# Attention with a conditioned residual: in the last slots the products for the maxima come by pairs of heads

## What is computed

```python
h = _layernorm(x)
mod = jax.nn.silu(time) @ mod_w + mod_b
shift, scale, gate = jnp.split(mod, 3, axis=-1)
h = h * (scale + 1.0) + shift
qkv = (h @ w_qkv).reshape(B, T, 3, H, e).transpose(2, 0, 3, 1, 4)
q, k, v = (qkv[0], qkv[1], qkv[2])
q = _apply_rope(_layernorm(q, q_norm_w), position)
k = _apply_rope(_layernorm(k, k_norm_w), position)
scores = jnp.einsum('bhqe,bhke->bhqk', q, k) / jnp.sqrt(jnp.asarray(e, q.dtype))
attn = jax.nn.softmax(scores, axis=-1)
o = jnp.einsum('bhqk,bhke->bhqe', attn, v)
o = o.transpose(0, 2, 1, 3).reshape(B, T, D)
return x + o @ w_out * gate
```

## Time and profile before

| | |
|---|---|
| median of three runs | 1695.15 us (1694.68 to 1695.43) |
| profiled execution, its own time | 1697.0 us |
| its span, first to last instruction | 1694.8 us |
| TensorE busy (matmul) | 1633.6 us, 96% of the span |
| VectorE busy | 1238.2 us, 73% |
| ScalarE busy | 997.5 us, 59% |
| GpSimd busy | 977.5 us, 58% |
| mean granted TensorE clock | 0.986 of full speed |

### The profile page before, as it was taken

How to read it: one execution, slowest core, us unless ns; L and a number is a source line. 1 busy time by engine, 2 the same in 40 slices (tenths; PEclk the granted TensorE clock), 3 DMA queues, 4 the chain that set the end, 5 groups by cost and what they waited for, 6 DMA issues and landing times.

```text
span 1694.8 us, 31070 instructions
## 1 busy us (share of the span) xinstructions
PE 1633.6 (96%) x11846; PEld 960.7 (57%) x11846; DVE 1238.2 (73%) x1541; ACT 997.5 (59%) x1484; POOL 977.5 (58%) x769
## 2 busy tenths in 40 slices
PE   5979999999999999999999999999999999999887
PEld 3745565565555556566556555555656655655344
DVE  8767777777777777777777777777777777776453
ACT  3436665666666656566566666665656656666552
POOL 0525466566666665656656666666665665666452
PEclk9979999999999999999999999999999999999899
DMA  6024455546546455555555555654645555454563
GB/s 219 26 62 94 107 124 116 137 110 145 116 104 153 109 125 128 125 118 119 138 115 128 128 122 117 133 125 109 147 113 118 132 118 136 108 122 103 125 137 106
DMA packets 55417, 204.25 MB, mean 121 GB/s; under 512 B 6872, under 2 KB 6872, under 8 KB 39144
## 3 DMA queue, kind: packets, MB, share of 16 engines
q0 software_dynamic: 18144, 132.13, 38.6%
q1 hardware_dynamic: 37128, 70.14, 13.0%
HBM read 53.25 MB, written 16.88 MB: 41 GB/s over the span
## 4 chain that ended last, share of the span: by engine, by line
PE 91%; DVE 4%; issue 1%; ACT 1%; DMA 1%; SPq 0%; POOL 0%; DVEq 0%; ACTq 0%
PE Y L339 33%; PE O L447 13%; PE SA L428 13%; PE Y L357 10%; PE SM L396 6%; PE MB L379 3%; PE SA L432 3%; PE Y L462 3%; PE SA L331 2%; DVE cst L1053 1%; PE SA L406 1%; ACT probs L806 1%; DMA probs<-in_L_cond_w_qkv_dram 1%; DMA probs<-probs 1%; DVE wqkv_lo L1096 0%
## 5 line engine op out<-in xcount | busy, mean ns | idle before, releaser
L1288 POOL TENSOR_TENSOR probs<-probs 128x2048 f32<-128x2048 f32 x62 | 285.4, 4603 | 313.3 <-DMA probs<-probs 313.3
L1053 DVE TENSOR_REDUCE cst<-SM 128x2 fp32r<-128x1024 f32 x256 | 313.9, 1226 | 144.4 <-PE MB L396 142.6
L806 ACT ACTIVATE probs<-SM 128x1024 f32<-128x1024 f32 x256 | 263.0, 1027 | 137.9 <-PE SM L432 123.2
L1053 DVE TENSOR_REDUCE cst<-MB 128x2 fp32r<-128x1024 f32 x256 | 311.5, 1217 | 0.0
L808 ACT ACTIVATE probs<-SA 128x1024 f32<-128x1024 f32 x256 | 260.2, 1016 | 0.0
L447 PE MATMUL O<-probs,vals 128*32 128x512 f32 x2048 | 255.3, 613 | 0.0
L339 PE MATMUL Y<-wqkv_hi,hT_lo 128*128 128x512 f32 x716 | 225.5, 410 | 0.4 <-DVE hT_lo L1037 0.4
L1261 POOL TENSOR_TENSOR pair_part<-rows,rope_pair 128x256 f32<-128x256 f32 x128 | 120.3, 940 | 169.4 <-DVE rows L1031 168.5
L339 PE MATMUL Y<-wqkv_hi,hT_hi 128*128 128x512 f32 x716 | 213.4, 420 | 0.0
L715 ACT ACTIVATE rows<-Y 128x512 f32<-128x512 f32 x121 | 72.4, 598 | 221.1 <-PE Y L339 221.1
L339 PE MATMUL Y<-wqkv_lo,hT_hi 128*128 128x512 f32 x716 | 201.5, 403 | 0.0
(11 more groups left out here) (221 smaller groups left out, 3448.5 us busy)
## 6 DMA issues: line engine op xcount, KB each, us to landing
probs<-probs POOLq DMA_DIRECT2D x126, 1024.0 KB, 7.1
xin<-in_x_dram SPq DMA_DIRECT2D x62, 256.0 KB, 2.6
xres<-in_x_dram SPq DMA_DIRECT2D x60, 256.0 KB, 2.6
out_dram<-xres SPq DMA_DIRECT2D x60, 256.0 KB, 5.8
shift_scale<-mod_rows SPq DMA_DIRECT2D x15, 512.0 KB, 3.7
gate<-mod_rows SPq DMA_DIRECT2D x16, 256.0 KB, 3.2
rows<-in_L_cond_mod_w_dram SPq DMA_DIRECT2D x2, 1024.0 KB, 9.0
probs<-in_L_cond_w_qkv_dram SPq DMA_DIRECT2D x2, 1024.0 KB, 13.1
```

The costliest lines, as they stand in the source:

```text
L806: act.activation(a[:, 2:4, :], SM[:], ACT.Exp).then_inc(s_exp, 1)
L1053: dve.tensor_reduce(heads[:, 2 * half:2 * half + 2, 0], (SM, MB)[half][:], AX.X, ALU.max, negate=True).then_inc(max_out, 1)
L1288: pool.tensor_tensor(total, total, part, ALU.add).then_inc(keys_summed, 1)
```

## The change

For the groups 59 to 63 the maxima product of a tile t is split in two, heads 0 and 1 and heads 2 and 3, and both pairs go to the two MB banks. The second pair waits until the first pair's maximum is read. The product with v that stood before the maxima product now stands between the pairs. At t = 0 the v projection stands there (slots 58 and 59), at t = 3 the product with v and a third of the output product. In slots 58 to 62 a key product after t = 0 no longer waits for maxima, and a maxima product no longer waits for exponentials. On ScalarE the high part of the outputs moves, in slots 59 to 62, from between the two exponentials of t = 0 to ahead of the high parts of q and k. The number of instructions on VectorE, ScalarE and GpSimd is the same. `SPLIT` is the first group whose maxima come by pairs; `qm_count` adapts the count that a maximum waits for.

```diff
--- before.py
+++ after.py
@@ -50,6 +50,9 @@
 
     def late(s):
         return s > NT - 7
+
+
+    SPLIT = NT - 5
 
 
 
@@ -210,8 +213,14 @@
         def head_rows(i):
             return slice(E * i, E * (i + 1))
 
-        def qm_bank(i):
-            return SM[:, i, :] if i < 2 else MB[:, i - 2, :]
+
+        def qm_bank(g, i):
+            return MB[:, i % 2, :] if late(g - 1) else SM[:, i, :] if i < 2 else MB[:, i - 2, :]
+
+
+        def qm_count(g, t, pair):
+            whole = min(g, SPLIT)
+            return TT * whole + 2 * TT * (g - whole) + (2 * t + pair + 1 if late(g - 1) else t + 1)
 
         def s_bank(i):
             return SA[:, i, :] if i < 2 else SM[:, i - 2, :]
@@ -379,6 +388,19 @@
                     mm = pe.transpose(MB[:, j, t * P:(t + 1) * P], rows[:, b % 2, t, j, i * P:(i + 1) * P], ident[:])
                 mm.then_inc(qkT_done, 1)
 
+            def scores_by_pair(g, t, pair):
+
+                n = TT * g + t
+                if t == 0 and pair == 0:
+                    pe.wait_ge(qk_low, 2 * g + 2)
+                pe.wait_ge(max_out, 2 * n + pair)
+                cols = slice(t * P, (t + 1) * P)
+                for i in (2 * pair, 2 * pair + 1):
+                    r = head_rows(i)
+                    mm = pe.matmul(qm_bank(g, i), qk_hi[r, g % 2, 0, cols], qk_hi[r, g % 2, 1, :],
+                                   start=True, stop=True)
+                mm.then_inc(qm_done, 1)
+
             def scores_by_query(g, t):
 
                 n = TT * g + t
@@ -393,7 +415,8 @@
                 cols = slice(t * P, (t + 1) * P)
                 for i in range(HG):
                     r = head_rows(i)
-                    mm = pe.matmul(qm_bank(i), qk_hi[r, g % 2, 0, cols], qk_hi[r, g % 2, 1, :], start=True, stop=True)
+                    mm = pe.matmul(qm_bank(g, i), qk_hi[r, g % 2, 0, cols], qk_hi[r, g % 2, 1, :],
+                                   start=True, stop=True)
                 mm.then_inc(qm_done, 1)
 
             def transpose_c(g):
@@ -415,7 +438,7 @@
                         pe.wait_ge(h_lo, 6)
                 if n > 0:
                     pe.wait_ge(s_exp, 2 * n)
-                if t == 0 or group(g + 1):
+                if t == 0 or not late(g):
                     pe.wait_ge(max_out, 2 * (n + TT - 1) + 1)
                 if t == 2 and tile(g + 6):
                     pe.wait_ge(h_hi, g + 7)
@@ -565,17 +588,25 @@
                 begun = 5 if s > 0 and not late(s - 1) else 0
                 if begun:
                     project_part(s + 4, 2, Y[:], 0, begun)
-                if group(s + 1):
+                if late(s) and group(s + 1):
+                    scores_by_pair(s + 1, 0, 0)
+                    if tile(s + 4):
+                        project_part(s + 4, 2, Y[:], begun, 9)
+                        begun = 9
+                    scores_by_pair(s + 1, 0, 1)
+                elif group(s + 1):
                     scores_by_query(s + 1, 0)
                 if s > 0 and tile(s + 4):
                     project_part(s + 4, 2, Y[:], begun, 12)
 
                 scores_by_key(s, 1)
                 if late(s):
-                    weigh_values(s, 0)
                     if group(s + 1):
-                        scores_by_query(s + 1, 1)
+                        scores_by_pair(s + 1, 1, 0)
+                        weigh_values(s, 0)
+                        scores_by_pair(s + 1, 1, 1)
                     else:
+                        weigh_values(s, 0)
                         add_last_sums(0)
                         add_over_keys(s - 1, MB[:, 1, :])
                     if s == LAST - 1:
@@ -607,8 +638,9 @@
                 scores_by_key(s, 2)
                 if late(s):
                     if group(s + 1):
+                        scores_by_pair(s + 1, 2, 0)
                         weigh_values(s, 1)
-                        scores_by_query(s + 1, 2)
+                        scores_by_pair(s + 1, 2, 1)
                         if tile(s + 4):
                             pe.wait_ge(v_out, s + 5)
                         pe.wait_ge(y_gated, n + 1 if s == LAST - 1 else n)
@@ -632,14 +664,17 @@
 
                 scores_by_key(s, 3)
                 if late(s):
-                    weigh_values(s, 2)
                     if group(s + 1):
-                        scores_by_query(s + 1, 3)
+                        scores_by_pair(s + 1, 3, 0)
+                        weigh_values(s, 2)
                         m = n + 1 if s == LAST - 1 else n
                         pe.wait_ge(o_low, m + 1)
                         pe.wait_ge(sum_ln, s)
-                        project_out(m, Y[:], 0, 12)
+                        project_out(m, Y[:], 0, 4)
+                        scores_by_pair(s + 1, 3, 1)
+                        project_out(m, Y[:], 4, 12)
                     else:
+                        weigh_values(s, 2)
                         add_last_sums(2)
                         pe.wait_ge(sum_ln, LAST)
                         pe.wait_ge(last_low, 2)
@@ -872,12 +907,12 @@
                 if s > 0 and tile(s + 5):
                     move_qk(s + 5, 1, Y[:])
                 move_c(s)
+                if late(s - 1) and s < LAST:
+                    output_high(s - 5)
                 if group(s + 1):
                     high_qk(s + 1, 0)
                     high_qk(s + 1, 1)
                 key_exponentials(s, 0, 0)
-                if late(s - 1) and s < LAST:
-                    output_high(s - 5)
                 key_exponentials(s, 0, 1)
                 if s > 0:
                     move_o(s - 1)
@@ -1046,11 +1081,12 @@
 
             def maximum(g, t, half):
 
-                dve.wait_ge(qm_done, TT * g + t + 1)
+                dve.wait_ge(qm_done, qm_count(g, t, half))
                 if t == 0 and g > 0:
                     dve.wait_ge(cT_done, g)
                 heads = cst[:, t, :].rearrange("p (h e) -> p h e", e=E)
-                dve.tensor_reduce(heads[:, 2 * half:2 * half + 2, 0], (SM, MB)[half][:], AX.X, ALU.max, negate=True
+                bank = MB if half or late(g - 1) else SM
+                dve.tensor_reduce(heads[:, 2 * half:2 * half + 2, 0], bank[:], AX.X, ALU.max, negate=True
                                   ).then_inc(max_out, 1)
 
             def maxima(g, t):
```

## The result

The changed kernel took 1697.47 us (median of 20 runs, 1695.08 to 1698.38), the kernel before 1694.74 in 20 runs beside it (1692.23 to 1698.21). The ratio is 1.0016, 95% interval 1.0010 to 1.0023: slower by 2.7 us (1.7 to 3.9). The forecast was slower by 5.3, 1700.4 us.

A forecast was written before the change was run, and what follows sets the result against it. The prediction took TensorE's chain to bound the kernel. Five slots sum to 111.0 against 104.8 us at 2.4 GHz: +6.2, less 4.6 and plus 3.7 for the clock, +5.3 on 1695.15, 1700.4 us; range 1695.0 to 1704.0.

The forecast's parts named there:

- Waits: Slots 58 to 62: the key product's 11.0 us of waits for maxima go; each pair waits for the one before.
- The round trip: Between pairs: product, maximum on VectorE and release take 1.91 us, two per step, 3.82 us where a step took 4.36.
- The pair's price: A two-head product on TensorE: 0.24 us beside a key product, 0.44 alone, 0.32 more inside a full-width product.
- The move: Outputs' high part earlier on ScalarE: first pair at 3.85 us, 0.13 late; 0.6 a slot less if left in place.
- Slot 58: VectorE's normalization comes between the maxima, TensorE stands some 2 us: 22.8 us, against 20.79 before.
- Slot 62: The 5.03 us chain from sums over keys to output product stays and starts later: 25.0 us, against 22.16 before.
- The clock: Slots 58 to 62: falls to 1.2 GHz cost 4.6 us before; after the change 2.4 falls at 1.53, 3.7 us.
- four stretches that it named: Places for clock falls: slot 58 before its last awaited pair; slots 60, 61, 62 between product with v and key product.
- The rival in which the clock stays up: First rival: no clock falls in the five changed slots, +1.6 us, 1696.7 us; chance 0.25.
- The rival of long falls: Each of four idle stretches brings a long clock fall at 2.9 us: +13.2 us, 1708.3 us; chance 0.07.
- The rival in which nothing takes the wait's place: Round trip hides behind TensorE's work, 11.0 us go, 4.8 of products come: -6.2 us, 1689.0 us; chance 0.08.
- The rule I had weighed: Trainium skill on TensorE's clock gate: warns only of gaps longer than any in the changed slots, so the clock stays up.

The follow-up runs named there:

- with fillers: The changed kernel plus products nobody reads where TensorE waits in slots 58, 60, 61 and 62, against the kernel before: 1693.64 us, ratio 0.9997.
- pairs in 59 to 61 and fillers: Kernel before with pairs only in slots 59 to 61, ScalarE's order as before, plus filler products in slots 58, 60, 61 and 62: 1689.85 us, ratio 0.9974.
- the kernel before with fillers: The kernel before plus four unread products at each of seven TensorE waits in slots 58 to 62: 1690.70 us, ratio 0.9976.
- the last experiment: Pairs in slots 59 to 61 plus filler products, with slot 62's outputs' high and low part made earlier, against the kernel before: 1689.76 us, ratio 0.9976.
- pairs from slot 59 on: The changed kernel with slot 58 (group 59) by four heads as before, against the kernel before: ratio 1.0008, +1.4 us.
- single heads: The changed kernel with each head's product and maximum by itself, each bank released by its own, against the kernel before: ratio 1.0000.
- the earlier high part: The changed kernel with slot 62's high part between the exponentials of t = 2 and low part ahead of the scaling, against the kernel before: ratio 0.9992, -1.4 us.

## Why the prediction was right, and where its size was off

*Waits.* The key product's wait went, and the pair's wait for the maximum before it took its place, in every slot. Moving the product with v out from between the pairs made it 13.6 us worse than the change and put a gap of 1.32 us into each step; releasing the banks one by one made slot 60 0.94 us shorter. So that wait is the bound between the pairs. That step held.

*The round trip.* Taken as 1.91 us, from a maxima product to the key product behind it; between pairs it is 1.82. p00 stood at 3.68 in slots 60 to 62 instead of 3.85: the low parts ended at 3.63, not 3.71, and the release took 0.05 us, not 0.14. So p21 came 0.6 us earlier than forecast in slot 60. This is the term that was mis-sized: with fillers the five slots sum to 108.3, the forecast was 111.0 (22.8, 22.0, 20.6, 20.6 and 25.0 against 22.26, 21.63, 20.07, 20.06 and 24.28). All five were put too long by it. In slot 58 there is a second error of the same sign: from the end of p11's maximum to the start of p20's VectorE took 2.17 us, not 2.36.

*The pair's price.* Taken as 0.24 beside a key product, and it is 0.21 to 0.22. In the run with v ahead of both pairs, a key product with a pair ahead of it went from 1599.86 to the product with v at 1601.21, 1.35 us, and in slot 60 of the change one with a pair behind it from 1605.67 to 1607.03, 1.36 us; alone it takes 1.14. The prediction had named any other price than 0.24 as a sign of being wrong; the miss is 0.02 to 0.03 us a pair. From p21 to the slot's end it came to 7.30 us, forecast as 7.2.

*The move.* Held: it starts the first pair later. Its cost, 0.3 to 0.4 us a slot, was within the bound of 0.6. It is also what the pairs gain in slots 59 to 61: at the upper clock level these three are no shorter in the change than before (+0.14, +0.01 and 0.00), and 0.85 us shorter together without the move.

*Slot 58.* Held, 22.26 forecast as 22.8: the normalization stands between the maxima, TensorE waits 1.90 us.

*Slot 62.* Held, 24.28 forecast as 25.0: the chain from the sums to the output product kept its 5.0 us and only began later.

*The end.* Left out. In the kernel before the last slot can wait for the accumulating DMA of slot 62 (0.81 us in its trace, 0.79 with pairs in 59 to 61 and fillers, none shown in the kernel before with fillers), so what slot 62 loses or gains is in part returned. In the change the wait is gone: 0.3 us of its loss come back against the filled kernel before, 1.1 against the kernel before itself. In the last experiment all of the gain goes, and more.

*The clock.* The forecast had the kernel before lose 4.6 us and the changed one 3.7. Measured with fillers they lose 4.1 (ratio 0.9976) and 3.2 (1.0016 less 0.9997), each with an interval of about 1.8 us on each side. The forecast of 3.7 for the change is right in part by luck. It had 2.4 falls at 1.53 us; the profile shows three at 1.23, again 3.7 together (111.99 less the 108.3 with fillers). And only two of the three, in slots 58 and 61, are among the four stretches that it named. The third came behind the wait for the low part in slot 62, 1.60 us, which the prediction forecast but didn't count as a place for a fall. The rival in which the clock stays up is out. The rival of long falls is out for the change (1708.3 against 1697.47), but long ones do come: slot 62 of three variants with pairs in it (pairs from slot 59 on, single heads, the earlier high part) ran at a mean clock of 0.86 or 0.87. The rival in which nothing takes the wait's place is out by the 17 waits. The rule I had weighed, by which only longer gaps bring the clock down, is not borne out here: the wait before p21 in slot 58 was 1.90 us, and the clock then fell.

So +3.6 in five slots, -0.3 to -1.1 at the end and -0.9 of clock make +1.6 to +2.4; measured 2.7 (1.7 to 3.9). Forecast: +6.2 and -0.9. The ratio's own forecast, 1.0031, lay above the interval; the miss of 2.6 us is that of the slots' sum. The direction and the waits came out as forecast, the size was half. The time alone, 1697.47, lies nearer to the first rival's 1696.7 than to 1700.4, and only the falls in the trace tell them apart. By the prediction's own classes, which call anything within 0.2% the same, 1.0016 belongs to "same" (0.32) and not to "slower" (0.60), though the interval leaves no doubt that the change is slower.

## What to carry to other kernels

Splitting a product to take a wait off one engine puts another wait in its place if the halves share their banks: each half waits for a full round trip through the reader (1.82 us here), unless the work between the halves is as long as that. Releasing each bank by itself made the trip 1.60. Apply such a change slot by slot: here it gained in the three slots with nothing else between the maxima (3.7 us, clock included, once the high part stood where it was before) and lost in the two where another engine's work or a dependent chain stood there. Count what a wait does to the clock as well as its length: filling TensorE's waits with products that nobody reads gained as much (4.1 us) as the best order without them (3.7), and both together hardly more (4.4). Before shortening a slot, look at what the next one waits for: here a DMA took the last gain back.

## What the hardware showed

- Products on different rows of the array start together: p01, on the rows of heads 2 and 3, and the key product's first two heads both at 1596.95. The pair is still paid, 0.21 to 0.22 us, at the key product's other end.
- From a maxima product to the product released by its maximum it took 1.91 us where a second maximum followed the first at once, and 1.82 where VectorE had nothing behind it. The difference lies between the end of the maximum and the product's start, 0.14 against 0.05 us. Whether the second maximum is the reason wasn't tried.
- The granted clock fell, from the level of 2.4 GHz to that of 1.2, in slots with gaps of 1.3 to 1.9 us between bursts of products, none longer. The same gap of 1.32 to 1.33 us had a fall behind it in slot 61 of the change and none in slots 60 and 62. With four products of 128x128 by 512 in each of the seven gaps of the kernel before the mean was 1.00 in all five slots, and that was worth 4.1 us of 1695.
- A maximum over 128x1024 takes 1.23 us, two over 128x512 1.29: the fixed part of a maximum from PSUM is small, 0.06 us back to back.
